# Attention on Trainium2: 32-row maximum products in two row groups, score banks by head

## The reference, cut to what matters

```python
# x: (1, 4096, 256); h = 8 heads of 32 features
attn = jnp.einsum('bhqd,bhkd->bhqk', q, k) * scale
attn = jax.nn.softmax(attn, axis=-1)
attn_out = jnp.einsum('bhqk,bhkd->bhqd', attn, v)
# then: attn_out through o_w, plus the output of a linear attention, plus x
```

## Time and profile before

| | before |
|---|---|
| median of 3 executions | 4649.83 us |
| the profiled execution, its span | 4658.0 us |
| first maximum product to first score | 2688.3 to 2739.6 us |
| the 1024 steps | 2739.6 to about 4633 us |
| busy from 2744.4 to 4633 us (1888.6 us): TensorE, VectorE, ScalarE | 1883.7, 1532.2, 1122.3 us |
| TensorE's granted clock in these steps | 1.00 |

### The profile page before, as it was taken

One profiled execution on the slowest core, in us unless ns is written; L12 is line 12 of the kernel. 1 busy time (PEld: TensorE's weight loads), 2 busy tenths in 40 slices (PEclk: granted clock), 3 DMA queues, 4 the chain that ended last, 5 costly groups with the idle time before them and its releaser, 6 DMA issues. The chain is left out here.

```text
span 4658.0 us, 151584 instructions
## 1 busy us (share of the span) xinstructions
PE 4395.0 (94%) x64527; PEld 2839.4 (61%) x64527; DVE 3292.1 (71%) x5448; ACT 1913.2 (41%) x2685; POOL 1037.3 (22%) x1042
## 2 busy tenths in 40 slices
PE   5999699999999999999968789999999999999998
PEld 4444499999999999996756624444444444444443
DVE  4899755655655655653459778787878888887876
ACT  2888411111111111110434426565655556565654
POOL 1000143343344344341047630000000000000000
PEclk9999899999999999999989979999999999999999
DMA  4544411111111111112344330000000000000000
GB/s 140 157 130 132 130 56 57 52 53 54 53 55 54 52 56 54 53 47 68 115 124 110 98 72 9 9 14 9 14 9 14 9 14 9 14 9 14 9 14 9
DMA packets 261652, 250.13 MB, mean 54 GB/s; under 512 B 51712, under 2 KB 230016, under 8 KB 260256
## 3 DMA queue, kind: packets, MB, share of 16 engines
q1 hardware_dynamic: 240528, 209.39, 15.0%
q0 software_dynamic: 6144, 16.79, 1.1%
q10 hardware_dynamic: 14352, 14.55, 0.9%
HBM read 135.27 MB, written 105.38 MB: 52 GB/s over the span
## 5 line engine op out<-in xcount | busy, mean ns | idle before, releaser
L2221 DVE TENSOR_REDUCE part_max<-p_m 128x1 f32<-128x512 f32 x2118 | 1364.1, 686 | 378.7 <-PE p_m L2063 371.2
L2203 ACT ACTIVATE prob<-p_s 128x1024 f32<-128x1024 f32 x1024 | 1047.8, 1023 | 749.2 <-PE p_s L2127 747.2
L2082 PE MATMUL p_o<-prob,v_one 128*64 128x512 f32 x4096 | 1054.4, 593 | 3.9 <-ACT prob L2203 0.5
L2063 PE MATMUL p_m<-keys,queries 96*64 96x512 f16 x4236 | 660.9, 387 | 27.9 <-DMA keys<-parts_d 20.3
L2127 PE MATMUL p_s<-queries,keys 97*64 97x512 f16 x4096 | 618.5, 380 | 0.0
L2127 PEld LDWEIGHTS p_s<-queries,keys 97*64 97x64 f16 x4096 | 227.1, 109 | 600.1 <-issue 594.6
L2063 PEld LDWEIGHTS p_m<-keys,queries 96*64 96x64 f16 x4236 | 238.2, 108 | 311.6 <-DVE part_max L2221 56.4
L848 PE MATMUL pd_pre<-inv,step 64*64 64x64 f32 x10240 | 384.4, 219 | 23.8 <-issue 22.1
L2031 POOL TENSOR_TENSOR attn<-o_num,o_inv 32x512 f32<-32x512 f32 x64 | 80.9, 1264 | 1458.5 <-DVE o_inv L2240 1452.0
L2082 PEld LDWEIGHTS p_o<-prob,v_one 128*64 128x64 f32 x4096 | 286.7, 136 | 163.7 <-issue 15.9
L848 PEld LDWEIGHTS pd_pre<-inv,step 64*64 64x64 f32 x10240 | 345.4, 135 | 57.4 <-issue 55.4
(11 more groups left out here) (245 smaller groups left out, 6612.8 us busy)
## 6 DMA issues: line engine op xcount, KB each, us to landing
q_d<-conv_q SPq DMA_DIRECT2D x16, 1024.0 KB, 5.0
v_d<-conv_v SPq DMA_DIRECT2D x16, 1024.0 KB, 5.0
k_d<-conv_k SPq DMA_DIRECT2D x16, 1024.0 KB, 6.5
sums<-sums_d SPq DMA_DIRECT2D x128, 128.0 KB, 3.0
k_t<-k_d SPq DMA_DIRECT2D x32, 512.0 KB, 4.6
q_t<-q_d SPq DMA_DIRECT2D x32, 512.0 KB, 3.4
v_t<-v_d SPq DMA_DIRECT2D x32, 512.0 KB, 3.4
slots_d<-zero ACTq DMA_DIRECT2D x1, 10112.0 KB, 32.5
```

The costliest lines, as they stand in the source:

```text
L2063: last = te.matmul(p_m[k % 2][x * HALF:(x + 1) * HALF, :], queries[0:ROW, p, hh, at:at + HALF], keys[0:ROW, 2 * p + hh, kb * BLK:(kb + 1) ...
L2082: product = te.matmul(p_o[64 * hh:64 * hh + VW, :], g.v_one[:, j, p, hh:hh + 2, :].rearrange("p a d -> p (a d)"), prob[:, j % 2, hh, :], s ...
L2203: a.activation(prob[:, j % 2], p_s[j % 2][:], ACT.Exp, scale=SCORE_SCALE).then_inc(exp_d, 1)
L2221: v.tensor_reduce(part_max[:, hh * SUB + sub, kb:kb + 1], p_m[k % 2][:], AX.X, ALU.max).then_inc(red_d, 1)
```

## The change

`NMAX` falls from 64 to 32 and `EARLY` from 6 to 2. A maximum product now covers 1024 keys and 128 queries: four matmuls of 32 rows and 64 columns, two of them in rows 0 to 31 and two in rows 64 to 95, the two row groups taking different blocks of 512 keys and writing different banks. It contracts the high parts alone (high·high); the maximum is only taken off the exponent and cancels in the softmax. A new tile `queries_low` holds the high part of the queries at partitions 64 to 95, with two more loads per pair of heads and block. `p_m` becomes two tiles of two banks. `p_s` becomes one bank per head: scores, waits and exponentials go head by head, each over 512 columns. Maximum products come in pairs at even steps only. The two biases are loaded into `out_tile` instead of tiles of their own.

```diff
-    NMAX = 2 * SUB * KB
+    NMAX = SUB * KB
     MAX_END = NKT - 3
-    EARLY = NMAX - 2 * MAX_END
+    EARLY = 2
+    UPPER = slice(0, DF)
+    LOWER = slice(2 * DF, 3 * DF)
...
+    queries_low = sb("queries_low", [P, HP, 2, BLK], F16)
...
-    part_max = sb("part_max", [P, 2 * SUB, KB])
+    part_max = sb("part_max", [P, 2 * SUB, KB // 2])
...
-    bias = sb("bias", [P, D])
-    nest_b = sb("nest_b", [P, D])
...
-    p_s = [ctx.enter_context(nc.psum_tensor(f"p_s{n}", [P, 2, BLK], F32)) for n in range(2)]
-    p_m = [ctx.enter_context(nc.psum_tensor(f"p_m{n}", [P, BLK], F32)) for n in range(2)]
+    bias, nest_b = out[:, 0, :], out[:, 1, :]
+    p_s = [ctx.enter_context(nc.psum_tensor(f"p_s{n}", [P, BLK], F32)) for n in range(2)]
+    p_m = [ctx.enter_context(nc.psum_tensor(f"p_m{n}", [P, 2, BLK], F32)) for n in range(2)]
...
-        start = EARLY + 2 * j if j < MAX_END else 2 * (j - MAX_END)
-        return range(start, start + 2)
+        if j % 2:
+            return ()
+        return (EARLY + j, EARLY + j + 1) if j < MAX_END else (0, 1)
...
+                sp.dma_start(queries_low[LOWER, p, hh, :], g.parts_d[c, at:at + DF, bass.ds(b * BLK, BLK)]).then_inc(q_in[p], 16)
...
-                last = te.matmul(p_m[k % 2][x * HALF:(x + 1) * HALF, :], queries[0:ROW, p, hh, at:at + HALF],
-                                 keys[0:ROW, 2 * p + hh, kb * BLK:(kb + 1) * BLK], start=True, stop=True)
+                for half, (rows, side) in enumerate(((UPPER, queries), (LOWER, queries_low))):
+                    first = (2 * kb + half) * BLK
+                    last = te.matmul(p_m[k % 2][x * HALF:(x + 1) * HALF, half, :], side[rows, p, hh, at:at + HALF],
+                                     keys[rows, 2 * p + hh, first:first + BLK], start=True, stop=True)
             last.then_inc(mm_d, 1)
...
-            if hh == 0:
-                if j == 0:
-
-                    pe.wait_ge(o_d, n)
-                pe.wait_ge(exp_d, n * NKT + (j + 1))
+            if hh == 0 and j == 0:
+                pe.wait_ge(o_d, n)
+            pe.wait_ge(exp_d, n * (2 * NKT) + (2 * j + hh + 1))
...
                 for j in range(NKT):
-
-                    pe.wait_ge(exp_d, n * NKT + (j - 1) if before is not None or p > 0 or j > 0 else 0)
                     for hh in range(2):
+                        if before is not None or p > 0 or j > 0:
+                            pe.wait_ge(exp_d, n * (2 * NKT) + (2 * j + hh - 1))
                         for x in range(2):
                             at = j * P + x * HALF
-                            last = te.matmul(p_s[j % 2][x * HALF:(x + 1) * HALF, hh, :], keys[0:KR, 2 * p + hh, at:at + HALF], queries[0:KR, p, hh, :],
+                            last = te.matmul(p_s[hh][x * HALF:(x + 1) * HALF, :], keys[0:KR, 2 * p + hh, at:at + HALF], queries[0:KR, p, hh, :],
                                              start=True, stop=True)
-                    last.then_inc(s_d, 1)
+                        last.then_inc(s_d, 1)
...
-                    act.wait_ge(s_d, n * NKT + (j + 1))
-                    a.activation(prob[:, j % 2], p_s[j % 2][:], ACT.Exp, scale=SCORE_SCALE).then_inc(exp_d, 1)
+                    for hh in range(2):
+                        act.wait_ge(s_d, n * (2 * NKT) + (2 * j + hh + 1))
+                        a.activation(prob[:, j % 2, hh], p_s[hh][:], ACT.Exp, scale=SCORE_SCALE).then_inc(exp_d, 1)
...
-            v.tensor_reduce(part_max[:, hh * SUB + sub, kb:kb + 1], p_m[k % 2][:], AX.X, ALU.max).then_inc(red_d, 1)
+            v.tensor_reduce(part_max[:, hh * SUB + sub, kb:kb + 1], p_m[k % 2][:].rearrange("p h t -> p (h t)"), AX.X, ALU.max).then_inc(red_d, 1)
```

More of the change, by code:

```diff
@@ L1927, in phase_attention @@
         sem(n) for n in ("lq_in", "base_in", "dens", "dene", "denr", "nums", "lin", "fin", "bb", "out", "out_out"))
-    LOADS = 6
+    KEY_LOADS = 6
+    QUERY_LOADS = 8
     READY = 3 * NB + sum(D >> (b * EX // NB) < D for b in range(NB)) + 2 * KC
@@ L1942, in max_steps, with max_place @@
     def max_steps(j):
-        start = EARLY + 2 * j if j < MAX_END else 2 * (j - MAX_END)
-        return range(start, start + 2)
-    def max_step(k):
+        if j % 2:
+            return ()
+        return (EARLY + j, EARLY + j + 1) if j < MAX_END else (0, 1)
+    def max_place(k):
         hh, rest = divmod(k, NMAX // 2)
-        return (hh,) + divmod(rest, KB)
+        return (hh,) + divmod(rest, KB // 2)
     block = ctx.enter_context(nc.Block())
@@ L1971, in _ @@
                                  (nest_o[:], g.given["nest_o_t"].rearrange("(c p) n -> p c n", p=P)),
-                                 (bias[:], g.given["lin_o_b"].partition_broadcast(P)), (nest_b[:], g.given["nest_o_b"].partition_broadcast(P))):
+                                 (bias, g.given["lin_o_b"].partition_broadcast(P)), (nest_b, g.given["nest_o_b"].partition_broadcast(P))):
                     sp.dma_start(dst, src).then_inc(w_in, 16)
@@ L1983, in one @@
             for p in range(HP):
-                sp.wait_ge(s_d, (b * HP + p + 1) * NKT)
+                sp.wait_ge(s_d, (b * HP + p + 1) * (2 * NKT))
                 load_queries(b + 1, p)
@@ L2053, in _, with max_products @@
         te = nc.tensor
-        def max_product(n, p, k):
-            hh, sub, kb = max_step(k)
+        def max_products(n, p, k):
+            hh, sub, kb = max_place(k)
             if k >= 2 or not isinstance(n, int) or n > 0:
@@ L2099, in final @@
             last.then_inc(fin_d, 1)
-        pe.wait_ge(q_in[0], 16 * LOADS)
-        pe.wait_ge(keys_in[0], 16 * LOADS)
+        pe.wait_ge(q_in[0], 16 * QUERY_LOADS)
+        pe.wait_ge(keys_in[0], 16 * KEY_LOADS)
         for k in range(NMAX):
-            max_product(0, 0, k)
+            max_products(0, 0, k)
         pe.wait_ge(cleared, 3)
         max_rows(0)
-        pe.wait_ge(q_in[1], 16 * LOADS)
-        pe.wait_ge(keys_in[1], 16 * LOADS)
+        pe.wait_ge(q_in[1], 16 * QUERY_LOADS)
+        pe.wait_ge(keys_in[1], 16 * KEY_LOADS)
         for k in range(EARLY):
-            max_product(1, 1, k)
+            max_products(1, 1, k)
         def one(b, before):
@@ L2121, in one @@
                 for j in range(NKT):
[L2123 removed]
                     for hh in range(2):
+                        if before is not None or p > 0 or j > 0:
+                            pe.wait_ge(exp_d, n * (2 * NKT) + (2 * j + hh - 1))
                         for x in range(2):
                             at = j * P + x * HALF
[L2127 removed]
+                            last = te.matmul(p_s[hh][x * HALF:(x + 1) * HALF, :], keys[0:KR, 2 * p + hh, at:at + HALF], queries[0:KR, p, hh, :],
                                              start=True, stop=True)
[L2129 removed]
+                        last.then_inc(s_d, 1)
                     if j == MAX_END:
[L2132 to L2133 removed]
+                        pe.wait_ge(keys_in[nxt2], 16 * KEY_LOADS)
+                        pe.wait_ge(q_in[nxt2], (b + 1) * (16 * QUERY_LOADS) if p < HP - 2 else (b + 2) * (16 * QUERY_LOADS))
                     for k in max_steps(j):
[L2136 removed]
+                        max_products(n + 1 if j < MAX_END else n + 2, nxt if j < MAX_END else nxt2, k)
                     for hh in range(2):
```

## The result

| | before | after |
|---|---|---|
| median of 12 executions each, on the same chip | 4652.14 us | 4660.91 us (4653.35 to 4670.83) |
| ratio | | 1.0018 [1.0010, 1.0027] |
| the profiled execution, its span | 4658.0 us | 4660.4 us |
| first maximum product to first score | 51.3 us | 39.5 us |
| first to last score of the loop | 1890.5 us | 1910.6 us |

The changed kernel is slower by 0.18%, 8.8 us. The forecast was 4648, 2 us under the runs of before. The last three lines of the table hold what the change did: -11.8 + 20.1 + 1.4 = +9.7 us. The two profiled spans differ by only 2.4, because in this pair the first maximum product came 7.3 us earlier (2681.0 against 2688.3), out of stages that the change does not touch.

The account below looks back on a forecast made before the run. The prediction took TensorE, busy 94% of the span, to bound the kernel. 4658.0 + 10 (loop) - 11.6 (before it) = 4656.4 us profiled, 4648.2 on the runs' scale; forecast 4648, no change, range 4605 to 4716.

Parts of the forecast that it names:

- -11.6 before the loop: Before the loop: 32 wide reductions replace 64 (-9.1 us), and the first score waits only for the copies (-2.5 us).
- The quad streams like a pair: Maximum products on TensorE: four matmuls take 0.22 us, like a pair, gaining 0.43 per two steps; upper bound 0.43.
- A change of tiling costs 0.09: TensorE between full-height products and 32-row quads: each change, in whichever direction, delays the next group by 0.09 us.
- late weights: TensorE after a change of tiling: first weights are not loaded ahead, adding 0.02 us to quads and 0.05 to values.
- the first rival: ScalarE: the two exponentials don't overlap, adding 0.13 us on 14 x 32 waits; +60 us, 4708, slower; chance 0.12.
- the wait is 0.07: After an odd step, head 1's scores wait for its previous exponential: +0.07 us on 14 of 16 pairs, +0.98 a round.
- -0.17: TensorE, a pair of steps inside a round: 3.28 us against 3.45 before, without the waits; 16 pairs give -2.72 a round.
- 0.98: Edge of a round, ScalarE: exponentials behind `copy_rows` delay the next round's scores, ending at 3.06 against 2.08 us.
- 1.28: Edge of a round, VectorE: the copy behind two wide reductions makes the new round's values wait 1.62 us, today 0.29 + 0.05.
- +0.52: Whole round with p = 2: -2.72 + 0.98 + 0.98 + 1.28 us, on a round of 56.04.
- I take +0.3 on average: +10 us for 32 rounds: Mean over all rounds of the loop: p = 1, 3 and 0 were taken as kinder than p = 2's +0.52 us.
- The schedule's own range: Whole program if the forecast's schedule holds, good to 0.02 us per pair of steps (10 us): 4636 to 4660, chance 0.46.

Follow-up runs that it names:

- rows96: Changed kernel with each maximum product in 96 rows, its two halves one after the other, without changes of tiling or row groups: 1.0195 times the kernel before.
- every_step: Changed kernel with one maximum product in each step instead of two in every second step: 1.0110 times the kernel before.

## Why the prediction was wrong

The forecast put two terms against each other, -11.6 before the loop and +10 in it, and called it no change. The sign hung on 10 us out of 4650.

**Right, by its own steps.** The quad streams like a pair: 0.22, with 0.24 for the first behind the other tiling (forecast 0.24 with its late weights). The rule of the Trainium skill (TensorE: Matmul & The Clock Gate, Part 3, "Measured speedup vs the span model") by which tiles of one pack cost a few nanoseconds each agrees with these 0.22 to 0.24. The measured 3.07 times that the Trainium skill gives in the same place is for four row tiles, a pack that no run here has; a loss of that share, 0.29 for a quad, does not show here. A change of tiling costs 0.09 in each direction, and 0.02 and 0.05 for late weights: rows96 and every_step give 0.26 for a visit by difference. The Trainium skill (TensorEngine Tiling (Array Packing), Key Properties) says that a change of tiling mode drains the array; the trace agrees in so far as the group behind each change starts 0.09 later. The odd step took 1.30 (1.29). The two exponentials overlap, 1.08 long together, so the first rival fell, and the wait is 0.07 as worked out, in seven blocks of eight. The wide reduction takes 1.22 alone and 1.14 in a row (1.14 to 1.23). The new round's first scores end 3.07 after the start of `max_rows` (3.06): from 3316.52 to the quad at 3319.68, less 0.09. Its first values come 1.62 late (1.62): by starts, 3321.14 + 0.43 to 3323.14 is 1.57, and late weights cost 0.05; the 1.40 printed leaves out the tail of the group before. Before the loop the change brought -11.8 (-11.6).

**Right, with small errors.** Take the round p = 2. Its steps 2 to 29 took 47.03 us after (3324.05 to 3371.08) and 48.35 before, -1.32 where 14 pairs at -0.17 and 13 waits at 0.07 make -1.47. Its steps 0, 1, 30 and 31 took 9.70 after and 7.69 before, +2.01 where -0.34 + 0.07 (the wait in step 30) + 0.98 + 1.28 makes +1.99. Together +0.69 against +0.52. Nearly all of the 0.17 is in the pairs: one took 3.364 (3.35), before 3.453 (3.45), 0.01 less gain than worked out, 13 times. 32 rounds make 5.4 us of it.

**The step that failed: "I take +0.3 on average: +10 us for 32 rounds".** The mean is +0.57, 18 us. Of the 0.27 that were missing, 0.17 are the small errors just named, which every round has. The other 0.10 (3 us) are a reading that was wrong. I expected the other rounds to be kinder, since small products "give ScalarE time, which saves two to four waits of 0.07 each", with p = 3 and with p = 0. It is true for p = 3, whose small products stand at j = 3 and j = 7: the even step after each has no wait. TensorE in p = 3, end of step 3 and scores of step 4 (matmul, weight load, matmul):

```profile
3384.17 1.13 PE L2167 MATMUL p_f<-lin_q,kv_block 128*128 128x512 f32 x2
3385.23 0.14 PEld L2132 LDWEIGHTS p_s<-queries,keys 97*64 97x64 f16 x4 [0.76 <-issue]
3385.23 0.62 PE L2132 MATMUL p_s<-queries,keys 97*64 97x512 f16 x4
```

All four weight loads of these scores come together, held by nothing but their issue, and the group is 0.62 long: no wait. It is not true for p = 0. Its small products stand at j = 20, 22, 24 and 26, in even steps. The wait is at the next even step, behind the exponential of the odd step between, and a piece in the even step gives that exponential nothing. The same view in p = 0, steps 20 to 22:

```profile
3473.06 1.03 PE L2102 MATMUL p_f<-nest_ob,attn 128*128 x4
...
3474.02 0.62 PE L2132 MATMUL p_s<-queries,keys 97*64 97x512 f16 x4
...
3475.33 0.68 PE L2132 MATMUL p_s<-queries,keys 97*64 97x512 f16 x4
```

The scores behind the products (3474.02, odd) never had a wait; the ones after (3475.33, even) are 0.68 long, as everywhere. So p = 0 gained nothing (+0.70), p = 3 two waits (+0.49), and p = 1 its old wait of 0.31 (+0.38). The loop measures +20.1; the 2 us beyond the 18 are the first block, +4.4 where a later one has +2.3, as its waits are 0.13 each: there the term "+0.07" itself was half of what it costs. Nor had I counted the end of the program, +1.4, where one piece of the output ran at the lower clock.

**The size of it.** The sum came out 11 us off (+9.7 against -1.6): about 5 and 3 in the rounds, 2 more in the first block, 1.4 at the end, less 0.2 before the loop. A round's result is a small difference (+0.69 for p = 2) of two larger terms, -2.6 for the quads and +3.3 for the waits, and an error of a few hundredths of a microsecond a wait comes back 32 times. The schedule's own range, 4636 to 4660, allowed for 10 us of such errors in the pairs of steps, and not for the reading of p = 0 or the first block; the measured 4660.9 lies just beyond it.

## What to carry to other kernels

When an operation is made cheaper by making it larger, list what stands behind it on every engine: here the gain of about 0.16 us a pair was real, and two buffers that came free later and one copy behind a wider reduction took all of it back. Price such a wait in each place where it comes: it was 0.07 in the loop and 0.13 in the block written out. Such waits are worth moving, since three changes of order, with no work removed, turned +0.2% into -2.2%. Where a wait falls in one step of two, only the work in the step just before it can hide it: small pieces are better placed by the parity of the wait (the pieces with p = 3 show it; moving those with p = 0 was not tried). And edits that each take a wait away need not add up: alone they saved 126.7 us, together 106.7.

## What was not expected of the hardware

Two exponentials of 128 partitions run 1.08 us long together (0.59 each), but two copies of one partition take 1.20 (3316.98) and two of 32 partitions 1.28 (3256.75): these small ones are the slow ones, as each begins only when the last has ended (0.02 us after). What about them does it, the few partitions or something else, no run here separates; that both are copies is not enough, as a copy of 128 partitions overlapped with what followed it. A change between full height and 32 rows cost the same 0.09 as one between 64 and 128 rows, with four tiles in use instead of two. And the quads of 32 rows stream together at the lower clock too: before the loop, at a granted clock of 0.50 (1.2 GHz), two quads started 0.43 us apart (2719.15 and 2719.58), where at 2.4 GHz it is 0.24 and 0.22.
